# The statistics of two layer norms: the first from VectorE to GpSimd, the second in interleaved pairs

## What is computed

```python
def _layernorm(x, axis=-1, eps=1e-05):
    m = jnp.mean(x, axis=axis, keepdims=True)
    v = jnp.var(x, axis=axis, keepdims=True)
    return (x - m) / jnp.sqrt(v + eps)
...
x = L0_attn_hidden_states
x = x + _L0_attn_ref(_layernorm(x, axis=-1), ...)   # 16 heads of 16 features, rotary on the last 256 tokens
x = x + _L0_ffn_ref(_layernorm(x, axis=-1), ...)    # top 128 tokens for each of 16 experts, and a shared expert
```

## Time and profile before

| what | value |
|---|---|
| median of three runs | 2369.97 us |
| the profiled execution's own time | 2370.57 us |
| its span | 2368.6 us |
| mean granted TensorE clock | 0.973 |
| TensorE (PE) busy | 2199.1 us, 93% |
| VectorE (DVE) busy | 1870.5 us, 79% |
| ScalarE (ACT) busy | 1560.5 us, 66% |
| GpSimd (POOL) busy | 932.4 us, 39% |
| row maxima, line 554, 2048 of them | 1280.4 us busy |
| exponentials, line 677, 2048 of them | 1120.4 us busy |

### The profile page before, as it was taken

How to read it: one execution, slowest core, us unless ns; L and a number is a source line. 1 busy time by engine, 2 the same in 40 slices (tenths; PEclk the granted TensorE clock), 3 DMA queues, 4 the chain that set the end, 5 groups by cost and what they waited for, 6 DMA issues and landing times. The chain is left out here.

```text
span 2368.6 us, 42180 instructions
## 1 busy us (share of the span) xinstructions
PE 2199.1 (93%) x15502; PEld 1274.5 (54%) x15502; DVE 1870.5 (79%) x3323; ACT 1560.5 (66%) x3056; POOL 932.4 (39%) x1372
## 2 busy tenths in 40 slices
PE   4899999999999999999999997899988999999996
PEld 3233333333333333333343223788877888888886
DVE  4899999999999999999999994566664555545553
ACT  2499889899899898998898886333323433434332
POOL 4051362462462461552552230000004666666664
PEclk8699999999999999999999998899998999999998
DMA  4002013113112122112112111422313454444543
GB/s 113 5 25 35 17 41 70 34 41 70 34 60 66 28 67 57 34 59 52 34 44 50 34 43 68 139 92 95 101 59 107 89 110 112 99 103 108 110 94 36
DMA packets 204837, 156.20 MB, mean 66 GB/s; under 512 B 110081, under 2 KB 185729, under 8 KB 204673
## 3 DMA queue, kind: packets, MB, share of 16 engines
q1 hardware_dynamic: 180096, 120.47, 18.4%
q0 software_dynamic: 24576, 33.57, 8.2%
HBM read 78.50 MB, written 50.33 MB: 54 GB/s over the span
## 5 line engine op out<-in xcount | busy, mean ns | idle before, releaser
L554 DVE TENSOR_REDUCE sb_MX<-ring 128x1 f32<-128x512 f32 x2048 | 1280.4, 682 | 60.3 <-PE ring L833 39.6
L677 ACT ACTIVATE sb_PR<-rot 128x512 f32<-128x512 f32 x2048 | 1120.4, 609 | 136.5 <-PE rot L844 120.6
L833 PE MATMUL ring<-sb_KT,sb_QT 32*128 32x512 bf16 x2048 | 517.4, 391 | 78.8 <-DVE sb_MX L554 63.2
L855 PE MATMUL pv<-sb_PR,sb_VA 128*32 128x512 f32 x4096 | 547.2, 606 | 2.3 <-ACT sb_OT L729 0.6
L833 PEld LDWEIGHTS ring<-sb_KT,sb_QT 32*128 32x128 bf16 x2048 | 126.5, 91 | 685.3 <-DVE sb_MX L554 626.5
L844 PE MATMUL rot<-sb_QT,sb_KT 32*128 32x512 bf16 x2048 | 405.3, 386 | 0.9
L1153 ACT ACTIVATE ex_GL<-ex_gu 128x512 f32<-128x512 f32 x128 | 76.4, 597 | 348.8 <-PE ex_gu L63 346.6
L1220 DVE TENSOR_TENSOR ex_HF<-ex_GL,ex_gu 128x512 f32<-128x512 f32 x128 | 87.5, 684 | 252.2 <-ACT ex_GL L1153 252.2
L1111 POOL DMA_INDIRECT out<-ex_YS,ex_rows_out x128 | 209.2, 1635 | 43.9 <-issue 43.5
L1068 POOL TENSOR_TENSOR ex_pool_scratch<-identity 128x1 f32<-128x1 f32 x96 | 35.1, 365 | 462.7 <-POOLq L910 316.8
L61 PE MATMUL ex_gu<-ex_XH,weights_high 128*128 128x512 f32 x512 | 201.1, 393 | 2.4 <-DVE ex_XL L1212 2.4
(11 more groups left out here) (163 smaller groups left out, 4022.5 us busy)
## 6 DMA issues: line engine op xcount, KB each, us to landing
sb_XA<-x SPq DMA_DIRECT2D x8, 1024.0 KB, 5.4
sb_XR<-x SPq DMA_DIRECT2D x8, 1024.0 KB, 5.6
out<-sb_XR SPq DMA_DIRECT2D x8, 1024.0 KB, 4.5
xn<-sb_XN SPq DMA_DIRECT2D x8, 1024.0 KB, 4.5
xn2T<-sb_XT SPq DMA_DIRECT2D x8, 1024.0 KB, 4.2
sh_XG<-xn2T SPq DMA_DIRECT2D x16, 512.0 KB, 5.4
sh_X<-out SPq DMA_DIRECT2D x16, 512.0 KB, 4.7
weights<-WgT SPq DMA_DIRECT2D x16, 512.0 KB, 4.1
```

The lines of the kernel that those rows point to most:

```text
L554: nc.vector.reduce_max(MX[:, unit % 2, half, j, qt % 4:qt % 4 + 1], ring[m % RING][:], AX.X).then_inc(ring_done, 1)
L677: out = nc.scalar.activation(PR[V % P_STEPS][:, j, :], R[:], ACT.Exp, scale=0.25)
L833: nc.tensor.matmul(ring[m % RING][:], QT[g][r, P * qt:P * qt + P], KT[g][r, 512 * half:512 * half + 512], start=True, stop=True, tile_posi ...
L855: out = nc.tensor.matmul(pv_bank[head(j), :], VA[b % 2][:, kt, 4 * g + j, :], PR[V % P_STEPS][:, j, :], start=(kt == 0), stop=(kt == TT - 1))
```

## The change

First norm: VectorE keeps it for sequence 0 alone. For the others GpSimd does all of it, in eight parts (`statistics`): it adds the two halves of a tile's features, and again, until the sum of the 256 remains (parts 0 to 2), subtracts the mean from `XA` (parts 3 and 4), squares half of the tiles, and sums the squares in the same way (parts 4 to 7). The parts stand in steps 0 to 3 and 6 to 9 of block 0 for sequence 1, and in steps 51, 53, 54, 55, 57, 58, 59 and 62 of block b for sequence b + 2. The inverse root follows in step 10 and step 63. In steps 13 to 16 only the multiplication is left.

Second norm: one `bn_stats` reads two tiles with their features interleaved, 512 elements, so that its separate figures for even and odd elements are those of the two tiles, and no `bn_aggr` follows. The variance is then the sum of squares over 256. The wait for the previous use of the statistics moves from step 25 to step 21. Head and tail do the same with four instructions.

To make room, several small tiles now share memory with the sums (`cs_in`, `rt1`, `rt2`), and `powers` with `shifted`; `rope` waits for GpSimd's own instructions first.

```diff
-        return nc.vector.tensor_scalar(tmp, var, EPS, None, ALU.add)
+        return nc.vector.tensor_scalar(tmp, squares, 1.0 / D, EPS, ALU.mult, ALU.add)
...
+    EARLY = (0, 1, 2, 3, 6, 7, 8, 9)
+    LATE = (51, 53, 54, 55, 57, 58, 59, 62)
...
+        stats = [sb(f"stats{n}", [P, TT // 2, 6], F32) for n in range(2)]
+        mean = [s[:].rearrange("p a (b n) -> p (a b) n", n=3)[:, :, 1:2] for s in stats]
+        squares = [s[:].rearrange("p a (b n) -> p (a b) n", n=3)[:, :, 2] for s in stats]
...
+            def fold(s, width, stop, out=None):
+
+                while width > stop:
+                    width //= 2
+                    own.wait(pool)
+                    to = out if out is not None and width == 1 else s[:, :, 0:width]
+                    own.inc(nc.gpsimd.tensor_tensor(to, s[:, :, 0:width], s[:, :, width:2 * width], ALU.add))
+
+            def statistics(b, part):
+
+                by_tile = sums[:].rearrange("p (t c) -> p t c", t=TT)
+                by_half = sums[:].rearrange("p (t c) -> p t c", c=H)
+                half = part // 2 % 2
+                i = slice(4 * half, 4 * half + 4)
+                if part == 0:
+                    pool.wait_ge(rope_done, 2 * ROPE_TILES * max(b, 1))
+                    pool.wait_ge(xa_in, 16 * (b + 1))
+                    own.inc(nc.gpsimd.tensor_tensor(by_tile, XA[:, :, 0:H // 2], XA[:, :, H // 2:H], ALU.add))
+                elif part == 1:
+                    fold(by_tile, H // 2, QUAD)
+                elif part == 2:
+                    fold(by_tile, QUAD, 1, average[:].unsqueeze(2))
+                    own.wait(pool)
+                    own.inc(nc.gpsimd.tensor_scalar(average[:], average[:], 1.0 / H, 1.0, ALU.mult, ALU.mult))
+                elif part == 3:
+                    own.wait(pool)
+                    for quarter in range(2):
+                        c = slice(2 * quarter, 2 * quarter + 2)
+                        own.inc(nc.gpsimd.tensor_tensor(XA[:, c, :], XA[:, c, :], average[:, c].unsqueeze(2).to_broadcast([P, 2, H]),
+                                                        ALU.subtract))
+                elif part == 4 or part == 6:
+                    own.wait(pool)
+                    own.inc(nc.gpsimd.tensor_tensor(by_half, XA[:, i, :], XA[:, i, :], ALU.mult))
+                    if part == 4:
+                        for quarter in range(2, 4):
+                            c = slice(2 * quarter, 2 * quarter + 2)
+                            own.inc(nc.gpsimd.tensor_tensor(XA[:, c, :], XA[:, c, :],
+                                                            average[:, c].unsqueeze(2).to_broadcast([P, 2, H]), ALU.subtract))
+                else:
+                    fold(by_half, H, 1, deviation[:, i].unsqueeze(2))
...
-                own.inc(nc.gpsimd.tensor_tensor(out[:, i, :], src[:, i, :], mv[n][:, i, 0:1].to_broadcast(shape),
-                                                ALU.subtract))
-                own.wait(pool)
+                if n:
+                    own.inc(nc.gpsimd.tensor_tensor(out[:, i, :], src[:, i, :], mean[n][:, i].to_broadcast(shape),
+                                                    ALU.subtract))
+                    own.wait(pool)
...
-                if more and S == 7:
-                    inverse_root(0, b + 1)
+                if b == 0 and S in EARLY:
+                    statistics(1, EARLY.index(S))
+                if b == 0 and S == EARLY[-1] + 1:
+                    inverse_root(0, 1)
+                if b + 2 < B and S in LATE:
+                    statistics(b + 2, LATE.index(S))
+                if b + 2 < B and S == LATE[-1] + 1:
+                    inverse_root(0, b + 2)
...
-            def gather_stats(src, tiles):
-
-                for i in tiles:
-                    own.inc(nc.vector.bn_stats(stats[:, i, :], src[:, i, :]))
...
+            def gather_stats(n, src, pair):
+
+                nc.vector.bn_stats(stats[n][:, pair, :], src[:, 2 * pair:2 * pair + 2, :].rearrange("p a c -> p c a")
+                                   ).then_inc(stats_ready[n], 1)
...
-                if more and S <= 3:
-                    if S == 0:
-                        dve.wait_ge(xa_in, 16 * (b + 2))
-                    gather_stats(XA, (2 * S, 2 * S + 1))
-                if more and S == 4:
-                    for h in range(2):
-                        dve.wait_ge(xn_ready[h], 2 * (b + 1))
-                if more and S in (4, 5):
-                    merge_stats(0, range(4 * (S - 4), 4 * (S - 3)), S == 5)
                 if prev and 21 <= S <= 24:
+                    if S == 21 and b > 1:
+                        for h in range(2):
+                            dve.wait_ge(xn2_ready[h], 2 * (b - 1))
                     dve.wait_ge(x1_ready, TT * (b - 1) + 2 * (S - 20))
-                    gather_stats(XR, (2 * (S - 21), 2 * (S - 21) + 1))
-                if prev and S == 25:
-                    for h in range(2):
-                        dve.wait_ge(xn2_ready[h], 2 * (b - 1))
-                    merge_stats(1, range(TT), True)
+                    gather_stats(1, XR, S - 21)
```

More of the change, by code:

```diff
@@ L215, in attention @@
         rstd_ready = [sem(f"rstd_ready{n}") for n in range(2)]
-        mv_ready = [sem(f"mv_ready{n}") for n in range(2)]
+        stats_ready = [sem(f"stats_ready{n}") for n in range(2)]
         xn_ready = [sem(f"xn_ready{h}") for h in range(2)]
@@ L418, in inverse_root @@
             def inverse_root(n, count):
                 y = rstd[n]
-                pool.wait_ge(mv_ready[n], count)
-                own.inc(nc.gpsimd.tensor_scalar(spread[:], mv[n][:, :, 1], EPS, None, ALU.add))
+                if n:
+                    pool.wait_ge(stats_ready[n], TT // 2 * count)
+                else:
+                    own.wait(pool)
+                own.inc(nc.gpsimd.tensor_scalar(spread[:], squares[n] if n else deviation[:], 1.0 / H, EPS, ALU.mult, ALU.add))
                 own.wait(pool)
@@ L506, in _ @@
             own.inc(nc.vector.memset(KP[:].rearrange("p g t j c -> p (g t j) c")[:, :, HD:HD + 3], -1.0))
-            def gather_stats(src, tiles):
-                for i in tiles:
-                    own.inc(nc.vector.bn_stats(stats[:, i, :], src[:, i, :]))
[L513 to L521, removed]
+            def gather_stats(n, src, pair):
+                nc.vector.bn_stats(stats[n][:, pair, :], src[:, 2 * pair:2 * pair + 2, :].rearrange("p a c -> p c a")
+                                   ).then_inc(stats_ready[n], 1)
             def newton(n, k):
                 own.wait(dve)
-                step = rsqrt_step(nc, k, rstd[n][:], nt1[:], nt2[:], mv[n][:, :, 1])
+                step = rsqrt_step(nc, k, rstd[n][:], nt1[:], nt2[:], squares[n])
                 if k == RSQRT_STEPS - 1:
@@ L535, in normalise @@
                 for i in range(TT):
-                    step = nc.vector.tensor_scalar(out[:, i, :], src[:, i, :], mv[n][:, i, 0:1], rstd[n][:, i:i + 1],
+                    step = nc.vector.tensor_scalar(out[:, i, :], src[:, i, :], mean[n][:, i], rstd[n][:, i:i + 1],
                                                    ALU.subtract, ALU.mult)
@@ L586, in _ @@
             dve.wait_ge(xa_in, 16)
-            gather_stats(XA, range(TT))
-            merge_stats(0, range(TT))
+            for pair in range(TT // 2):
+                gather_stats(0, XA, pair)
+            dve.wait_ge(stats_ready[0], TT // 2)
             for k in range(RSQRT_STEPS):
@@ L607, in _ @@
                 b, S = V // STEPS, V % STEPS
-                more, prev = 0 <= b < B - 1, b > 0
+                prev = b > 0
                 m = 4 * (V + LEAD)
@@ L650, in _ @@
                 dve.wait_ge(xn2_ready[h], 2 * (B - 1))
-            for i in range(4):
-                dve.wait_ge(x1_ready, TT * (B - 1) + 2 * i + 2)
-                gather_stats(XR, (2 * i, 2 * i + 1))
-            merge_stats(1, range(TT))
+            for pair in range(TT // 2):
+                dve.wait_ge(x1_ready, TT * (B - 1) + 2 * pair + 2)
+                gather_stats(1, XR, pair)
+            dve.wait_ge(stats_ready[1], TT // 2 * B)
             for k in range(RSQRT_STEPS):
```

18 lines of the change are left out of this document (11 added, 7 removed).

## The result

The changed kernel takes 2351.77 us (median of four runs, 2349.01 to 2354.57) against 2369.76 us before (four runs, 2367.12 to 2370.20). The ratio is 0.9925, with a 95% interval of 0.9913 to 0.9937: 18 us faster. The profiled execution took 2354.57 us (span 2352.2), 2.8 over the median, so the two profiled spans stand 16.4 us apart (2368.6 to 2352.2). The four runs lie in two pairs (2349.0 twice at a mean granted clock of 0.976, 2354.5 twice at 0.972). What a single block takes is therefore read from its stretches, not from the total.

A forecast was written before the change was run, and what follows sets the result against it. VectorE was taken to lead in the attention stage, TensorE following closely. Terms 13.2 + 1.4 + 2.8 + 1.75 = 19.2 us, from 2370.6 to 2351.4, 2350.8 against the median, stated as 2351.0; range 2343 to 2368.5.

The forecast's parts named there:

- Step 1: First norm leaves VectorE, blocks 0 to 6: 2.20 us per block, 13.2 us for blocks 1 to 6, 1.4 in block 0.
- The 1.2 us that TensorE takes back: Middle blocks: of 3.4 us of first-norm work taken from VectorE, 2.20 show and TensorE takes back 1.2.
- Block 0's start: First norm's relief at block 0's start, mostly at 1.2 GHz: 1.4 us, between 0.5 and 2.2; step 2's statistics pair hidden.
- the prediction's fourth rival: Half-clock stretches at the attention stage's start and end move: 1 to 3 us either way; forecast including it 0.74.
- Step 2: Second norm in pairs, blocks 1 to 7: 0.4 us of some 0.9 per block, 2.8 us in all, between 0 and 6.
- The cover named: Step 24: TensorE waits for the next batch's last turned quarter, split on GpSimd; second-norm statistics lie in that shadow.
- half rate: Rival: interleaved statistics reads at half rate, 1.13 us per 512 elements, gain only 2.2 us (2368); chance about 0.08.
- Step 3: Serial statistics in head and tail: 2.5 us replace 3.36 and 3.42, gaining 0.85 + 0.9 = 1.75 us.
- Step 4: GpSimd's added work, some 140 us in the stage, costs 0, between -1 and 10 us; step 60's splitting about 1.4 late.
- my 20.5 us: New GpSimd work for one batch in the first norm's eight parts, out of 24.7 us altogether.
- the predicted 5.7: Slack in us by which step 60's splitting of the maxima on GpSimd may be late before TensorE stops.

## Why the prediction was right, point by point

**The bound** was read rightly: VectorE's work counts in steps 59 to 11, and not in full, since TensorE is next: removing the first norm's half alone (2.64 us of statistics, and the merges) made those steps 2.22 us shorter.

**Step 1, right.** Predicted 41.4 us from step 59 to step 11, measured 41.40; the worth of 2.20 us read from block 7 came out as 2.22 (22.20 + 21.42 - 20.66 - 20.74). Reading it from a block that lacks the work was better than pricing the work at 3.4 us. The 1.2 us that TensorE takes back are there: eight statistics of 0.33 give 1.85.

**Block 0's start, not seen in this profile.** The sum had 1.4 us. In the profiled executions, 25.92 + 21.24 us for its first two stretches became 25.26 + 21.84, a gain of 0.06. VectorE waits more often and longer for TensorE than in the earlier trace rows (in order of time, VectorE of the kernel after):

```profile
92.30 2.48 DVE L604 TENSOR_REDUCE sb_MX<-ring 128x1 f32<-128x512 f32 x4 [1.31 <-PE ring L874]
96.09 1.29 DVE L604 TENSOR_REDUCE sb_MX<-ring 128x1 f32<-128x512 f32 x2 [1.31 <-PE ring L874]
```

In this stretch the granted clock is 0.51, the 1.2 GHz level, and it lasts until 99.7 us in the kernel after and 99.0 before. The first stretch gains 0.65 of the 1.4, the second loses it again. But four of the runs above (gates in step 60, the square in step 61 with either place of the gates, the four more squares) change nothing before step 59 of block 0, so that these two stretches are the same work as in the kernel after, and there they take 46.10, 44.21, 44.22 and 45.83 us, against 47.10 after and 47.16 before: gains of 1.1 to 3.0 us. The full clock comes back at 97.6, some 92 (twice) and 96.9 us in them, and at 99.7 in the kernel after. So VectorE's work alone does not fix the term; where the full clock comes back does too, and that differs between profiles of the same work. That is the prediction's fourth rival, of 1 to 3 us either way. The profile of the change happens to be the one with the least gain, so its 0.1 us does not refute the 1.4.

**Step 2, right.** Predicted 22.9 us from 19 to 27 and 0.4 us per block; measured 22.98 and 0.34, seven blocks 2.4 for 2.8. The cover named is in the trace: TensorE's longest wait there, for its weights of the last turned quarter (the profile gives it to ScalarE, but GpSimd's split of that quarter ends at 1187.23, the last thing in front of it), is 1.01 us before the change and 1.06 after. TensorE's weight loads, before and then after:

```profile
1187.34 0.19 PEld L61 LDWEIGHTS rot<-sb_WH,sb_XH 128*128 128x128 f32 x1 [1.01 <-ACT sb_PR L677]
```

```profile
1172.11 0.19 PEld L61 LDWEIGHTS rot<-sb_WH,sb_XH 128*128 128x128 f32 x1 [1.06 <-ACT sb_PR L718]
```

Two sizes behind it were off. The eight merges of step 25 cost 0.55 us from start to start (1191.21 to 1191.76 before), not 0.6 to 0.75, and the statistics instruction 0.62 us, not 0.60; so 0.71 us of work went, not 0.9, and 0.34 of it shows. By the Trainium skill, Advanced Engine Details and Errata, section Memory Cachelines, reads that each meet a different line pay a penalty. The trace shows 0.02 us for 512 reads that take turns between two tiles, which is no half rate. Since each tile is read in order, such reads come back to a line that they have just met; reads that meet a new line each time and never return stand here only in the copy of 8 elements of the earlier trace rows, so the rule itself is not decided.

**Step 3, right.** 0.90 and 0.90 us for 0.85 and 0.9.

**Step 4, right in its worth, wrong in its sizes.** GpSimd's busy time grew by 117 us in the stage, not 140, and parts 1 to 6 took 16.5 us, not 17.9. One reason is the price of the square: I took the form with two different operands, which by the earlier trace rows makes 2.35 us for 1024 elements, but with the same operand twice it takes 1.89. Twice 0.46 us are 0.9 of the 1.4 by which parts 1 to 6 were too dear, and 6.4 us over seven sequences. The other is in the reckoning: my 20.5 us held the 0.08 us in front of each dependent instruction, 27 new ones in a batch and so 15 us in all, which busy time leaves out. Of the 143 us that seven times 20.5 makes, this leaves 122 for the measured 117; the last 5 were not traced. The splitting was not 1.4 us late but on time. The run with four more squares gave a slack of 5.5 us for the predicted 5.7.

**What was missing: the collisions.** I costed GpSimd's new work by its place in GpSimd's order alone, and asked only who waits for it. While it reads it can also hold up VectorE, as the run with added reads shows, and the edit put reading instructions beside two VectorE instructions with two inputs: 0.24 us in each of five blocks, and once more where block 0 ends and the joining of its step 59 runs into a square. GpSimd, then VectorE, of the kernel after:

```profile
243.46 1.89 POOL L459 TENSOR_TENSOR sb_sums<-sb_XA 128x1024 f32<-128x1024 f32 x1
...
244.64 0.74 DVE L610 TENSOR_TENSOR sb_MX<-sb_MX 128x16 f32<-128x16 f32 x1
```

That is 0.74 for 0.18, of which 0.21 shows in the next stretch (20.87 for 20.66; TensorE was next anyway): 5 x 0.24 + 0.2 = 1.4 us in all. The trace of before had it to be read. Its joinings take 0.17 or 0.18 us, but the one of step 35 takes 0.47, beside a multiplication of `normalise` (GpSimd, then VectorE, of the kernel before):

```profile
1217.03 1.04 POOL L442 TENSOR_TENSOR sb_XN<-sb_XN,sb_rstd 128x512 f32<-128x512 f32 x1
...
1217.63 0.47 DVE L560 TENSOR_TENSOR sb_MX<-sb_MX 128x16 f32<-128x16 f32 x1
```

It ends at 1218.10, just after GpSimd's 1218.07. One look at why the same instruction has two durations would have given the mechanism.

**The sum.** By the joinings of the profiled pair, predicted and measured:

| part | predicted | measured |
|---|---|---|
| up to block 0's first joining (head) | 0.85 | 1.4 |
| block 0 | 1.4 | 0.1 |
| blocks 1 to 6 | 15.6 | 14.0 |
| block 7 | 0.4 | 0.6 |
| tail | 0.9 | 0.9 |
| stages behind the attention | 0 | -0.6 |
| together | 19.2 | 16.4 |

Of the 1.6 us missing in blocks 1 to 6 the collisions are 1.4. The head's statistics gave 0.90 us; the other 0.5 in its row was not traced to an instruction, and it is within what the first joining moves by itself: with the head of the kernel before it stands at 73.52, 73.43, 72.94 and 72.60 us in four profiles. The profiled execution after lies 2.8 us over its median, and the one before 0.8: that is why the median came within 0.8 us of the forecast though the sum over the profiled pair missed by 2.8, and part of that closeness is chance. Runs of one kernel lie up to 6.2 us apart (2352.07 to 2358.24 for the first norm alone), and the slower ones have the lower granted clock (0.972 against 0.976); what causes that wasn't tested.

## What to carry to other kernels

To price work taken from an engine that only partly leads, look for a repetition of the loop that lacks it and take the difference between fixed points: it holds the next limit already. Price an instruction by a row with the same operands, not only the same size. And work that is put on an idle GpSimd must be laid against the other engine's order of time as well as its own: where it reads many elements, keep it clear of VectorE's short instructions with two inputs, by a wait if there is slack for one.

## What was unexpected of the hardware

A VectorE instruction with two inputs that came in the middle of a GpSimd instruction reading 512 or 1024 elements ended only after that one: 0.29 us became 0.55 and 0.85, 0.17 became 0.47, 0.74 and 0.82, and each ended 0.03 to 0.15 us after GpSimd's. A memset on GpSimd holds up nothing, and row maxima, with one input and that from PSUM, keep their mean of 683 ns (682 before) beside 117 us more of GpSimd's work. The Trainium skill has this rule, SBUF — State Buffer, section Who interferes with whom: a VectorE instruction with two SBUF inputs contends with GpSimd instructions that read SBUF, not with those that only write. The runs above agree.

It does not hold for every GpSimd instruction that reads, though, and the traces of before and after both show the exception. In the inverse root GpSimd takes a power of 8 elements, with two inputs from SBUF, for 1.65 us. The joining of step 27 comes 1.19 us into it, takes its usual 0.17 us and ends before it. GpSimd, then VectorE, of the kernel after:

```profile
669.38 1.65 POOL L477 TENSOR_TENSOR sb_rstd<-sb_spread,sb_minus_half 128x8 f32<-128x8 f32 x1
```

```profile
670.57 0.17 DVE L610 TENSOR_TENSOR sb_MX<-sb_MX 128x16 f32<-128x16 f32 x1
```

So it is not the length of GpSimd's instruction by itself that counts. That the few elements were already read by then would explain it, but no run parts the two. The other order, VectorE first and GpSimd held up, is shown by none of these rows. The longest hold measured is 0.68 us (a joining of 0.85 us, with the gates in step 60); that it can reach the whole 1.89 us of a square of 1024 elements is an estimate from where these instructions ended.

GpSimd multiplies 1024 elements by themselves in 1.89 us; adding two different halves of as many (part 0 of the change) takes 2.36. Whether the multiplication has a part in that was not tested apart.
